# Router-weight rows of a fused ViT layer: issued by ScalarE three steps ahead, instead of by the sync engine five steps ahead

## What is computed

```python
pooled = x.reshape(B, C, 14, 16, 14, 16).sum(axis=(3, 5))
h = einsum('bcij,ce->bije', pooled, channel_weights)      # 196 tokens of 192
h = h + attn(layernorm(h), proj_w, proj_b)                # 64 queries, 132 keys
# ffn, x2 = layernorm(h): router picks 2 of 8 experts per token
cw = zeros(T, 8); cw[t, indices] = weights
y = einsum('tei,edi,te->td', silu(x2 @ w1.T) * (x2 @ w3.T), w2, cw)
z = (silu(x2 @ sw1.T) * (x2 @ sw3.T)) @ sw2.T             # shared expert
return h + y + z
```

## Time and profile before

| | |
|---|---|
| median of 3 runs | 1950.12 us (1940.26 to 1956.4) |
| profiled execution | 1956.01 us, its span 1954.3 us |
| PE / DVE / ACT / POOL busy | 83% / 56% / 47% / 36% of the span |
| granted TensorE clock, mean | 0.909 |
| DMA, share of the 16 engines | 61.6% for the sync engine's queue |

### The profile page before, as it was taken

How to read it: one execution, slowest core, us unless ns; L and a number is a source line. 1 busy time by engine, 2 the same in 40 slices (tenths; PEclk the granted TensorE clock), 3 DMA queues, 4 the chain that set the end, 5 groups by cost and what they waited for, 6 DMA issues and landing times.

```text
span 1954.3 us, 30301 instructions
## 1 busy us (share of the span) xinstructions
PE 1616.2 (83%) x9350; PEld 1262.1 (65%) x9350; DVE 1096.3 (56%) x1863; ACT 919.6 (47%) x3047; POOL 702.9 (36%) x687
## 2 busy tenths in 40 slices
PE   2715759987898789987898879987998879999988
PEld 1204538855786577855686667855786567867877
DVE  6845656557464766557456665567456663246233
ACT  2334446555474545644374545644474543433123
POOL 4335325223522334223332334323432334324344
PEclk9855669889998989989999899989999899989999
DMA  8887766667676676667666676657766672123233
GB/s 307 309 319 283 282 232 245 239 228 262 231 280 217 231 274 252 241 222 263 216 257 229 227 265 250 252 209 269 259 252 236 234 267 70 45 92 107 89 99 95
DMA packets 120850, 436.58 MB, mean 223 GB/s; under 512 B 20109, under 2 KB 49538, under 8 KB 99182
## 3 DMA queue, kind: packets, MB, share of 16 engines
q1 hardware_dynamic: 120470, 434.10, 61.6%
q10 hardware_dynamic: 216, 0.50, 0.1%
HBM read 413.86 MB, written 20.07 MB: 222 GB/s over the span
## 4 chain that ended last, share of the span: by engine, by line
PE 41%; DMA 17%; issue 13%; DVE 13%; POOL 7%; SPq 5%; ACT 2%; ACTq 0%; DVEq 0%; POOLq 0%
PE bank L1426 15%; DMA ffn<-cw_rows 13%; PE bank L1275 11%; POOL ffn L654 5%; DMA xt<-in_x 5%; DVE pooled L841 4%; PE bank L1446 3%; DVE ffn L1189 3%; POOL stat L629 2%; SPq L481 2%; PE bank L1372 2%; PE bank L1384 1%; SPq L461 1%; PE bank L1344 1%; PE bank L1333 1%
## 5 line engine op out<-in xcount | busy, mean ns | idle before, releaser
L654 POOL TENSOR_TENSOR ffn<-ffn 128x512 f32<-128x512 f32 (+1 forms) x448 | 512.8, 1149 | 1020.1 <-ACT ffn L803 653.2
L1426 PE MATMUL bank<-W2T,ffn 128*128 128x192 f32 (+1 forms) x3600 | 717.5, 339 | 0.0
L1189 DVE TENSOR_TENSOR ffn<-bank,ffn 128x512 f32<-128x512 f32 (+1 forms) x504 | 313.2, 622 | 696.9 <-POOL ffn L654 499.8
L1426 PEld LDWEIGHTS bank<-W2T,ffn 128*128 128x128 f32 (+1 forms) x3600 | 619.9, 195 | 50.5 <-issue 12.4
L803 ACT ACTIVATE ffn<-bank 128x512 f32<-128x512 f32 (+1 forms) x504 | 274.6, 547 | 441.9 <-PE bank L1446 278.6
L841 DVE TENSOR_REDUCE pooled<-xt 128x5 f32<-128x1280 f32 (+2 forms) x296 | 434.4, 1471 | 41.9 <-DMA xt<-in_x 40.9
L699 ACT ACTIVATE xt<-xt 128x256 f32<-128x256 f32 x800 | 322.9, 410 | 128.6 <-DMA xt<-in_x 128.3
L1446 PE MATMUL bank<-tokT,Wx 126*128 126x512 bf16 (+1 forms) x720 | 247.5, 365 | 97.6 <-DVE ffn L1189 97.1
L1446 PEld LDWEIGHTS bank<-tokT,Wx 126*128 126x128 bf16 x720 | 73.0, 102 | 180.6 <-DVE ffn L1189 134.1
L699 ACT ACTIVATION_READ_ACCUMULATOR xt<-xt 128x1 f32 x800 | 155.4, 194 | 0.0
L1275 PE MATMUL bank<-x0h,WT0h 128*128 128x512 f32 x288 | 142.3, 494 | 12.2 <-issue 5.7
(11 more groups left out here) (245 smaller groups left out, 1841.1 us busy)
## 6 DMA issues: line engine op xcount, KB each, us to landing
xt<-in_x SPq DMA_DIRECT2D x168, 1792.0 KB, 7.4
ffn<-cw_rows SPq DMA_DIRECT2D x384, 256.0 KB, 7.5
out<-stage SPq DMA_DIRECT2D x192, 96.0 KB
ffn<-cw_rows SPq DMA_DIRECT2D x64, 32.0 KB, 6.7
ffn<-in_L_ffn_w SPq DMA_DIRECT2D x2, 768.0 KB
attw<-in_L_ffn_w SPq DMA_DIRECT2D x1, 512.0 KB
Wx<-tokT ACTq DMA_DIRECT2D x9, 54.2 KB
out<-stage SPq DMA_DIRECT2D x8, 48.0 KB
```

The lines of the kernel that those rows point to most:

```text
L654: nc.gpsimd.tensor_tensor(out=cwb[slot][:, 0:n], in0=silu[(g.par + step) % 2][:, 0:n], in1=cwb[slot][:, 0:n], op=ALU.mult).then_inc(scaled, 1)
L1189: v.tensor_tensor(out=h[step % HR][:, 0:n], in0=h_ps(g, step, 1)[:, 0:n], in1=(silu[p] if e == NE else cwb[(c * NE + e) % CW_RING])[:, 0:n ...
L1426: last = mm(o, h[step % HR][:, 128 * t:128 * t + m], W2T[:, e, :], start=(e == 0 and query and t % 2 == 0), stop=(e == NE), skip_group_che ...
```

## The change

ACT now stores the router weights, right after each of its seven copies, behind a wait for its own copy. ACT also issues the loads: at step s, after silu of that step (and after the evacuation of an earlier chunk's output where one stands there) it issues the load for step s+3. SP keeps the tile loads and the output stores. `CW_AHEAD` goes from 5 to 3; the ring of seven buffers stays.

```diff
-CW_AHEAD = 5
+CW_AHEAD = 3
...
-            def cw_rows_out(g, step):
-
-                for kind, i in items_at(step):
-                    if kind == "C":
-                        n = 512 if i < 6 else 64
-                        sp.wait_ge(aux_act, g.at(BYACT[-1], BYACT[R[("C", i)]]))
-                        sp.dma_start(cw_rows[g.par, :, 512 * i:512 * i + n], cw_stage[i][:, 0:n])\
-                          .then_inc(cw_out[1 if i else 0], 16)
-
-            def cw_load(g, step):
...
                     nc.scalar.copy(cw_stage[i][:, 0:n], ps[0:NE, 0:n]).then_inc(aux_act, 1)
+                    act.wait_ge(aux_act, g.at(BYACT[-1], BYACT[r]))
+                    act.dma_start(cw_rows[g.par, :, 512 * i:512 * i + n], cw_stage[i][:, 0:n])\
+                       .then_inc(cw_out[1 if i else 0], 16)
+
+            def cw_load(g, step):
...
+                def slot_free(use):
+
+                    back = use - CW_RING
+                    wait(act, h_done, g.at(STEPS, back // NE * EX + back % NE + 1))
+
+                if use == 0:
+                    act.wait_ge(cw_out[0], g.at(16, 16))
+                elif use == NE:
+                    act.wait_ge(cw_out[1], g.at(96, 96))
+                else:
+
+                    slot_free(use + 1 if use + 1 in (NE, CW_USES) else use)
+                at = col if query else 1024 + col
+                act.dma_start(cwb[slot][:, 0:n], cw_rows[g.par, e, at:at + n].partition_broadcast(128))\
+                  .then_inc(cw_landed[slot], 16)
...
                     nc.scalar.activation(silu[p][:, 0:n], h_ps(g, step, 0)[:, 0:n], ACT.Silu).then_inc(silu_done, 1)
                     if e == 1 and c > 2:
                         evacuate(g, c - 1)
+                    cw_ahead(g, step, left)
                     step_act(g, step, left)
```

More of the change, by code:

```diff
@@ L537, in ffn_dma @@
                         load_after(gt_, t)
-                    cw_ahead(g, step, left)
                     if e == 3 and c > 0:
@@ L547, in _ @@
                     load_after(gt_, t)
-                cw_ahead(G(None, -1), step, 1)
             ffn_dma(G(None, 0), 2)
@@ L764, in item, with cw_ahead @@
                     nc.scalar.copy(cw_stage[i][:, 0:n], ps[0:NE, 0:n]).then_inc(aux_act, 1)
+                    act.wait_ge(aux_act, g.at(BYACT[-1], BYACT[r]))
+                    act.dma_start(cw_rows[g.par, :, 512 * i:512 * i + n], cw_stage[i][:, 0:n])\
+                       .then_inc(cw_out[1 if i else 0], 16)
+            def cw_load(g, step):
+                c, e = divmod(step, EX)
+                if e == NE:
+                    return
+                query, col, n = CHUNKS[c]
+                use = c * NE + e
+                slot = use % CW_RING
+                def slot_free(use):
[10 more added lines that the diff above has]
+                  .then_inc(cw_landed[slot], 16)
+            def cw_ahead(g, step, left):
+                if step + CW_AHEAD < STEPS:
+                    if g.off >= 0:
+                        cw_load(g, step + CW_AHEAD)
+                elif left:
+                    cw_load(g.plus(1), step + CW_AHEAD - STEPS)
             def keys_out(dst, src, i):
@@ L810, in _ @@
             for step in range(A_FIRST, STEPS):
+                cw_ahead(G(None, -1), step, 1)
                 step_act(G(None, -1), step, 2)
```

## The result

The changed kernel takes 1883.73 us (median of 4 runs, 1878.09 to 1887.77), the kernel before in the same measurement 1949.11 (4 runs, 1940.26 to 1956.4). The ratio is 0.9664, with a 95% interval of 0.9613 to 0.9716: 3.4% faster. The forecast was 1885. The profiled execution took 1887.49 us, its span 1885.7, and the mean granted clock of TensorE was 0.924 (1956.01, 1954.3 and 0.909 before).

The account below looks back on a forecast made before the run. It took late router weight loads, held up by tile transfers on SP's queue, to bound the kernel. Terms -77 + 7 + 3 + 2 = -65 us gave 1891 for the profiled execution, 1885 us as median; range 1838 to 1938.

Parts of the forecast that it names:

- What bounds the kernel: Groups 0 to 5: image tiles cost 21.2 us a group, in chunks 3 to 6, visibly by holding up router weight loads.
- Part 1: Router loads leave SP's queue for ACT, landing in 4 to 6 us: 12.9 us a group, 77 us less in six.
- Chunk 3: Chunk 3 of groups 0 to 5: from 24.9 to 20.4 us, a gain of 4.5 a group.
- Chunks 4 to 6: These chunks in groups 0 to 5: from 87.4 to 79.0 us, 5 left for tile sums, gain 8.4 a group.
- Part 3: Router weight stores on ACT: 1 us in each of seven groups, 7 us, plus 3 us once ahead of group 0.
- Part 2: Load issues in ACT's stream: each 0.365 us issue is covered by a silu of 0.6 us, cost 0.
- Part 4: Lead of three where steps are short, group 7's chunk 3: 2 us lost.
- Part 5: SP without router loads: tile loads go out when their slot is free, output stores remain between; cost and gain 0.
- B: Rival: loads land no sooner on ACT, landing stays at 8.3 us; about 1936 us, no change; chance 0.12.
- D: Rival: three steps are too few, loads behind a tile land in 11.5 us; about 2055 us, slower; chance 0.06.
- C: Rival: ACT's issues are not covered, 14.6 us a group in key steps, 102 us; 1987 us, slower; chance 0.06.
- What would show it: Signs in the new profile: POOL's router waits under 80 us, landing below 6, chunk times, ACT's issue idle, SP's waits, clock.

Follow-up runs that it names:

- e3: Kernel before, all DMAs on SP, lead five, each tile load four steps later in SP's stream: 1922.90 us, ratio 0.9879.
- e9: Kernel before, all DMAs on SP, tile loads four steps later in SP's stream only from step 19 on (key chunks): 1876.15 us, ratio 0.9628.
- e5: Kernel before with each tile load from group 2 on cut to a sixteenth, sums still over the whole slot: 1861.62 us, one run.
- e6: Changed kernel with each tile load from group 2 on cut to a sixteenth, sums still over the whole slot: 1865.99 us, one run.
- e4: Changed kernel with only the stores of router weights back on SP, loads staying on ACT three ahead: 1870.07 us, ratio 0.9606.
- e7: Changed kernel with every load of router weights issued as two halves, 448 more issues on ACT: 1908.30 us, ratio 0.9795.
- e12: From e4, loads on ACT five steps ahead, the next group's first three issued together at step 60: 1881.30 us, ratio 0.9658.
- e1: Changed kernel with the loads five steps ahead on ACT instead of three: 1922.39 us, ratio 0.9882.
- e2: Kernel before with a lead of three steps instead of five, loads still on SP: 2530.21 us, ratio 1.3001.

## Why the prediction was right

**What bounds the kernel.** Right. Of 21.2 us that tiles cost a group, the changed kernel wins 11.5. The three views (chain, waits, windows with and without tiles) led to the right chunks. "Query chunks and chunk 2 cannot give much" was nearly right: they gave 1.0 and 1.1 us a group, 12.5 in six. Two things the text passed over. "TensorE covers the landing" was not so: of the 366.5 us that POOL waited for router weights, 57.7 lay in chunk 2 and 30.7 in the query chunks of groups 0 to 5, and they are gone. And the sum has no term for the granted clock, with which 29 us of the gain go. DVE, which the text has at "60% or less", is at 56.18/86.70 = 65% in the earlier trace rows.

**Part 1, the mechanism.** Right. The text gave two reasons, the shrunken lead and the tile ahead on the same queue, and weighed one against the other. Either alone can be taken away: e3 and e9 keep the tile ahead and restore the lead, e5 keeps the lead and shortens the landing, and chunks 4 to 6 take 79.1 to 79.2 us in all three. "About 8 us" of lead is 8.5 in the median, and the landing of 4 to 6 was met with 5.4. How the gain divides between the two is open.

**Chunk 3:** 20.4 forecast, 20.1 measured. **Chunks 4 to 6:** 79.0 forecast, 82.9 measured; this term is mis-sized. Its part for the tile sums, 5 us, is right (5.3 in e5). What it set to zero, "nearly all waits go", is 2.5 us of transfers (e6), and the stores of Part 3 fall into it too, 1.6 (e4). Six groups gave 27.5 us here where 8.4 x 6 = 50.4 were counted. Of this, 12.5 came back in the query chunks and chunk 2, and the store term of 6 lies inside the 27.5: the total owes its closeness partly to errors that cancel.

**Part 2, issues cost 0.** Right for one issue behind a silu: 2.0 us of idle time are put down to it in the steps. Where three stand in a row, ahead of group 0, they cost 2.8 us, which the text had at nothing although its own showed ACT idle for issues in a row. e7 puts an added issue at up to 0.055 us, 25 us for 448; how much of that lies in the changed kernel is open, since a second issue behind the first is not the same as the first behind a silu. e9's chunks 4 to 6 (79.1) are 2.1 us a group shorter than e4's (81.2), 13 us in six; whether issues have a part in that is not shown, as the leads differ too.

**Part 3, stores:** 7 + 3 us forecast, 13.7 measured by e4, of which 10.7 lie in groups 0 to 5. The step "ACT waits for TensorE's transposes between copies anyway" failed: the wait for its own copy leaves ACT idle 0.40 to 0.47 us, more than the 0.29 of the issue that I had counted. The first silu begins 4 us later where 3 were forecast, and the reason was another: 2.8 of the 4 are issues of loads, not stores.

**Part 4:** 2 us forecast, 2.7 measured (e12 gives them back). **Part 5,** nothing on SP: SP waited 231.9 us in 131 waits for DVE ahead of a router load before; these are gone. It now waits for tile slots, in the two rows below, and for finished outputs (L481), 350.7 us instead of 52.0. That this costs nothing is argued from the chunks' times, not tested:

```profile
SPq L230 <- ACT xt L654: 587.9, 130, 17.4
SPq L461 <- DVE pooled L833: 514.3, 151, 9.7
```

**The rivals.** B is excluded by its own condition, landings that stay at 8.3 us (5.4 measured), as well as by 1884 against 1936; D by landings of at most 8.2 us in chunks 4 to 6 of group 3, below its 9.3, and by a time that fell; C by e7. A rival that I had not named was the real danger: a longer lead on ACT, which looks safer, puts a wait for a landing into the stream of a compute engine (e1). With a lead of five the same change would have kept 1.2% instead of 3.4%.

**What would show it.** POOL's waits 32.2 (below 80), landing 5.4 (below 6), chunk 3 at 20.1, and the clock in chunks 4 to 6 of group 3 0.94 (0.92 before): met. Chunks 4 to 6 near 79, query chunks at 81 to 82, no idle time of ACT put down to issue and SP waiting for slots alone: missed, with 82.9, 80.7, 4.8 us and the waits for outputs.

## What to carry to other kernels

A prefetch of n steps is worth what its issuer's stream leaves of it: read when a load was really issued against when it was used, set that against how long it takes to land, and look for waits of other transfers ahead of it. A longer real lead and a sooner landing each help (e3, e5). Either give the loads an issuer without such waits or write the other transfers later in the same stream, which here gave the same. On a compute engine put only issues whose waits are already covered. Here a wait for a landing (4.65 us, e1) and one for the engine's own last copy (0.40 to 0.47 us) stopped what stood behind them, and the stores were better placed on the sync engine (e4).

## What I had not expected of the hardware

An issue on ACT took 0.331 us (SP: 0.365) and began ahead of activations that stand before it, as at 1061.15; 448 added issues cost at most 0.055 us each (e7). A wait for its own last copy took that cover away and cost 0.40 to 0.47 us. And a lead that another wait eats up costs far more than one late load for each tile: e2 lost 581 us, POOL's waits for router weights rose from 366.5 to 1071.2 us, TensorE was busy 70% of the span instead of 83%, and the granted clock was 0.831 instead of 0.909.
